# A Mamba layer with one-query attention on one core: filler products at the chunk borders, and jobs beside the scan moved by half states

## What is computed

```python
x = x + mamba(keep_largest_rows(x, sigmoid(cond @ score_w)))
x = x + ffn(attention(x, cond, mask))

# mamba, per sequence, 512 inner channels, 16 states
xi, z = split(rmsnorm(x) @ in_proj)
xi    = silu(causal_conv4(xi) + conv_b)
dt, Bm, Cm = split(xi @ x_proj)
delta = softplus(dt @ dt_w + dt_b)
h_s   = exp(delta * A_s) * h_s(before) + (delta * xi) * Bm_s     # 16 states s
y     = sum_s(h_s * Cm_s) + xi * D
out   = x + (y * silu(z)) @ out_proj

# attention: the same query for all rows of a sequence
qmod  = sum over rows of (tp . q) q ;  tp = cond @ Wt
o     = softmax(qmod . k) v @ Wo
```

## Time and profile before

| | |
|---|---|
| three runs | 529.36 us median (528.08 to 532.32) |
| the profiled execution, its own time | 528.79 us |
| its span, first to last instruction | 527.0 us |
| mean granted TensorE clock, as a share of full speed | 0.950 |
| before the loop's first scan | 42.88 us |
| chunks 0, 1, 2, 3 (first scan to first scan) | 113.10, 107.12, 103.77, 100.04 us |
| after the last scan | 60.09 us |

### The profile page before, as it was taken

One profiled execution on the slowest core, in us unless ns is written; L12 is line 12 of the kernel. 1 busy time (PEld: TensorE's weight loads), 2 busy tenths in 40 slices (PEclk: granted clock), 3 DMA queues, 4 the chain that ended last, 5 costly groups with the idle time before them and its releaser, 6 DMA issues.

```text
span 527.0 us, 8185 instructions
## 1 busy us (share of the span) xinstructions
PE 446.8 (85%) x2881; PEld 336.5 (64%) x2881; DVE 448.4 (85%) x527; ACT 380.3 (72%) x673; POOL 382.2 (73%) x235
## 2 busy tenths in 40 slices
PE   7967798887958999989789999896899778989991
PEld 6443665565648656766676667665888666878750
DVE  3779799989998899999998999999997998871153
ACT  4685688899966798898867988998676788741210
POOL 5139967986999579879996799799977999620001
PEclk9998899998997999999989999999997898899996
DMA  8531111111103111110110111101200295019205
GB/s 274 169 123 40 42 40 41 40 45 40 41 0 115 40 46 42 39 45 0 42 58 29 47 55 44 54 7 35 81 40 1 64 363 225 1 40 360 71 1 164
DMA packets 18422, 39.58 MB, mean 75 GB/s; under 512 B 1943, under 2 KB 10775, under 8 KB 18376
## 3 DMA queue, kind: packets, MB, share of 16 engines
q1 hardware_dynamic: 18376, 39.00, 21.3%
HBM read 36.76 MB, written 2.23 MB: 74 GB/s over the span
## 4 chain that ended last, share of the span: by engine, by line
PE 37%; DVE 34%; issue 16%; ACT 11%; POOL 1%; DVEq 0%; ACTq 0%; POOLq 0%
DVE scanmem L1951 22%; PE hT L974 7%; DVE yTd L1962 6%; PE pp L597 4%; PE pp L698 4%; PE yacc L668 4%; ACT dA L1442 3%; PE dA L936 2%; ACT hc L1452 2%; PE pp L766 2%; DVE yTd L1876 2%; PE pp L620 1%; PE pp L908 1%; PE pp L627 1%; DVE par L1742 1%
## 5 line engine op out<-in xcount | busy, mean ns | idle before, releaser
L1604 POOL TENSOR_TENSOR scanmem<-par,scanmem 128x1024 f32<-128x1024 f32 x128 | 300.1, 2365 | 57.6 <-PE hT L974 37.9
L974 PE MATMUL hT<-con,scanmem 128*128 128x128 f32 x1008 | 158.1, 287 | 49.3 <-DVE yTd L1962 35.5
L1442 ACT ACTIVATE dA<-par,Aneg 128x512 f32<-128x512 f32 x256 | 171.7, 690 | 36.0 <-DVE scanmem L1951 34.5
L974 PEld LDWEIGHTS hT<-con,scanmem 128*128 128x128 f32 x1008 | 118.1, 146 | 95.5 <-DVE yTd L1962 31.5
L1951 DVE TENSOR_TENSOR_SCAN scanmem<-dA,carry,scanmem 128x512 f32<-128x512 f32 x128 | 156.4, 1266 | 9.5 <-ACT dA L1442 8.1
L1951 DVE TENSOR_TENSOR_SCAN scanmem<-dA,scanmem 128x512 f32<-128x512 f32 x128 | 148.8, 1204 | 4.9 <-ACT dA L1442 3.2
L1452 ACT ACTIVATE hc<-hT,CTs 128x512 f32<-128x512 f32 x127 | 86.1, 678 | 25.4 <-PE hT L974 24.0
L668 PE MATMUL yacc<-con,hc 128*128 128x128 f32 x512 | 83.7, 290 | 0.0
L1962 DVE SCALAR_TENSOR_TENSOR yTd<-hT,CTs,yTd 128x512 f32<-128x512 f32 x90 | 65.4, 727 | 4.9 <-PE hT L974 2.5
L668 PEld LDWEIGHTS yacc<-con,hc 128*128 128x128 f32 x512 | 65.9, 151 | 0.2
L597 PE MATMUL pp<-xnT,wi 128*128 128x512 f32 x120 | 57.8, 609 | 4.1 <-DVE par L1742 2.4
(11 more groups left out here) (229 smaller groups left out, 527.9 us busy)
## 6 DMA issues: line engine op xcount, KB each, us to landing
scanmem<-brow SPq DMA_DIRECT2D x32, 512.0 KB, 3.6
par<-in SPq DMA_DIRECT2D x1, 4096.0 KB, 19.3
scanmem<-in SPq DMA_DIRECT2D x1, 4096.0 KB, 14.3
xt<-in SPq DMA_DIRECT2D x4, 512.0 KB, 6.9
wi<-in SPq DMA_DIRECT2D x2, 1024.0 KB, 7.9
out<-par SPq DMA_DIRECT2D x3, 512.0 KB, 3.9
aw<-in SPq DMA_DIRECT2D x5, 256.0 KB, 7.6
xr<-in SPq DMA_DIRECT2D x1, 1024.0 KB, 10.0
```

The costliest lines, as they stand in the source:

```text
L974: last = nc.tensor.transpose(hT[:, i % 2, m * P:(m + 1) * P], hb[:, n % RING, m, i * P:(i + 1) * P], ident)
L1442: A(dA[:, m % 2, :], delta(c)[:, m, :], ACT.Exp, scale=Aneg[:, m * NS + s:m * NS + s + 1]).then_inc(da_ready, 1)
L1604: nc.gpsimd.tensor_tensor(hb[:, n % RING, ms, :], dx(c)[:, ms, :], Bb[:, row:row + 1, :].to_broadcast([P, 2, T]), ALU.mult).then_inc(bx_re ...
```

## The change

The hand-written tables are changed; no product of the computation itself is added or left out.

1. In chunks 1 and 2 the next chunk's rows are turned at half 2 where it was half 3, and the first input product comes at half 3 where it was half 4 (`LATER_ROWS`).
2. A new job KW: six products of the identity with itself, 128x128, into the job's bank, read by nobody (the fifth frees the bank). It stands at halves 29, 31 and 32 of chunk 0 and at 31 and 32 of chunks 1 and 2 (half 32 is half 0 of the next chunk): seven jobs, 42 products.
3. U is moved from half 3 to half 30 of chunk 0.
4. `kept_rows` on POOL is moved from step 16 to step 18.
5. In chunk 3 the four O jobs stand one by one at halves 4, 5, 6 and 7 (it was two and two at 4 and 6), and A, G, A, G follow at 8, 9, 10, 11 (it was 7, 8, 8, 10).
6. SP waits for the last O in place of the second pair before it loads `H1` (its queue comes to that place after all of chunk 3's B rows).

```diff
+LATER_ROWS = {2: [("T", 0), ("T", 1)], 3: [("I", 0)], 4: [], 5: [("I", 1)]}
-LAST_EPILOGUE = {1: [("Y", 1)], 2: [("Y", 3)], 4: [("O", 0)], 6: [("O", 1)], 17: [("R", 0)], 19: [("R", 1)]}
-ATT = [7, 8, 8, 10, 12, ...
+LAST_EPILOGUE = {1: [("Y", 1)], 2: [("Y", 3)], 4: [("O", 0)], 5: [("O", 2)], 6: [("O", 1)], 7: [("O", 3)], 17: [("R", 0)], 19: [("R", 1)]}
+ATT = [8, 9, 10, 11, 12, ...
-KEPT_AT = NS
+KEPT_AT = NS + 2
+IDLE_AT = [(29, 31, 32), (31, 32)]
 def prologue_slots(n):
-    return slots(PROLOGUE if n > 1 else {**PROLOGUE, **FIRST_STEPS}, n)
+    return slots({**PROLOGUE, **(LATER_ROWS if n > 1 else FIRST_STEPS)}, n)
...
-            beside[3] += [("U", 0, 0)]
+            beside[30] += [("U", 0, 0)]
...
+            for k, h in enumerate(IDLE_AT[min(c, 1)]):
+                beside[at + h] += [("KW", c, k)]
...
+WARM_IDLE = 6
...
-            wait_full(sp, ("O", NCH - 2, 1))
+            wait_full(sp, ("O", NCH - 2, NT - 1))
...
+            def job_KW(job, o):
+
+                keep_warm(WARM_IDLE - 2, o[:, 0:P])
+                mm(o[:, 0:P], ident, ident, start=True, stop=True).then_inc(freed(job), 1)
+                return mm(o[:, P:2 * P], ident, ident, start=True, stop=True)
```

More of the change, by code:

```diff
@@ L58 @@
 FIRST_STEPS = {17: [("XT", 0)], 18: [("D", 0)], 19: [("D", 1)], 20: [], 21: [("D", 2)], 22: [("D", 3)]}
+LATER_ROWS = {2: [("T", 0), ("T", 1)], 3: [("I", 0)], 4: [], 5: [("I", 1)]}
 EPILOGUE = {1: [("Y", 1), ("Y", 3)], 15: [("O", 0)], 17: [("O", 2)], 18: [("O", 1)], 23: [("O", 3)], 28: [("R", 0)], 30: [("R", 1)]}
-LAST_EPILOGUE = {1: [("Y", 1)], 2: [("Y", 3)], 4: [("O", 0)], 6: [("O", 1)], 17: [("R", 0)], 19: [("R", 1)]}
-ATT = [7, 8, 8, 10, 12, 14, 15, 16, 18, 20, 22, 23, 25, 26, 28]
+LAST_EPILOGUE = {1: [("Y", 1)], 2: [("Y", 3)], 4: [("O", 0)], 5: [("O", 2)], 6: [("O", 1)], 7: [("O", 3)], 17: [("R", 0)], 19: [("R", 1)]}
+ATT = [8, 9, 10, 11, 12, 14, 15, 16, 18, 20, 22, 23, 25, 26, 28]
 ATT1 = [24, 27]
@@ L689, in job_O @@
                     pe.wait_ge(half_ready, 3)
[L690 to L698, removed]
+                t0 = j * P
+                if j % 2:
+                    wait_read(pe, ("Y", e, j))
+                else:
+                    pe.wait_ge(gated, 2 * e + j // 2 + 1)
+                for m in range(CT):
+                    last = mm(o[:, 0:DM], dx(e)[:, m, t0:t0 + P], wo[:, m, :], start=m == 0, stop=m == CT - 1)
                 return last
@@ L739, in job_R @@
                 wait_read(pe, ("O", e, j))
-                if e != NCH - 2:
-                    wait_read(pe, ("O", e, j + 2))
+                wait_read(pe, ("O", e, j + 2))
                 return turn_rows(o, e, j)
@@ L936, in keep_warm @@
                     mm(dst, ident, ident, start=True, stop=True)
+            def job_KW(job, o):
+                keep_warm(WARM_IDLE - 2, o[:, 0:P])
+                mm(o[:, 0:P], ident, ident, start=True, stop=True).then_inc(freed(job), 1)
+                return mm(o[:, P:2 * P], ident, ident, start=True, stop=True)
+            jobs["KW"] = job_KW
             def wait_free(job):
@@ L1762, in ev_O @@
                 _, e, j = job
[L1763 to L1766, removed]
+                g = e * NT + j
+                return V.scalar_tensor_tensor(xt[:, g, :], xt[:, g, :], keep1[:, g:g + 1], o[:, 0:DM], ALU.mult, ALU.add)
             def ev_AX(job, o):
```

## The result

| | before | after |
|---|---|---|
| median of 7 runs each | 530.05 us (526.81 to 532.32) | 524.65 us (522.73 to 525.63) |
| ratio | | 0.990, 95% interval 0.9868 to 0.9933 |
| profiled execution, span | 528.79, 527.0 us | 525.63, 523.8 us |
| mean granted clock | 0.950 | 0.954 |
| before the first scan | 42.88 us | 44.06 us |

The change makes the kernel 1.0% faster, 5.4 us between the medians; 523.9 had been forecast, a gain of 5.5 us on a median that was then 529.36. It loses 1.18 us ahead of the first scan and 1.30 us behind the last one (61.39 us, 60.09 before), where the change has touched nothing; the loop between them is 418.38 us, not 424.03, so 5.65 us shorter.

A forecast was written before the change was run, and what follows sets the result against it. No engine bounds it everywhere (VectorE and TensorE both 85% busy); VectorE's idle time inside the loop can be won. 0.9 + 1.17 + 0.9 + 0.5 + 2.4 - 0.4 = 5.5 us off 528.79, plus 0.57: 523.9 us, range 519.9 to 527.8.

The forecast's parts named there:

- U: Step 2: without U ahead of it T starts earlier and VectorE's wait for block 1 shrinks; 0.9 us, bounds 0.5 and 1.22.
- kept_rows: Step 15: with kept_rows behind POOL's sum, VectorE's whole wait for that sum goes; 1.17 us, bounds 0.6 and 1.17.
- The forecast's sentence on the clocks: Opening paragraph: granted clock 0.55 in step 16, 0.76 in step 32, 0.67 in step 52, 1.00 where nothing is said.
- Borders, T and I together: Chunk borders and following steps: 0.9 us gained at chunk 1's start, 0.5 at chunk 2's, less 0.4 for KW and U.
- The walk: Steps 32 to 35: T waits for VectorE to read Y; step 34 starts about 0.5 us later, step 35 at 284.0, not 284.24.
- the gate's waits: Steps 16 and 32: VectorE waits 0.76 and 0.73 us for the gate's sum; KW should hold the clock and remove both.
- Chunk 3: Step 52: spreading O, A and G wins 2.4 us of VectorE's 3.24 us wait; bounds 0.7 and 3.4.
- the rule: Step 52: transposes don't count for the clock as products do, so the low clock is sure and the term 1.6 us.
- All 3.24 us are won: Step 52 at the full clock: block 0 is there at 395.5 and VectorE's whole wait goes; 3.24 us.
- T is not held: Rival, steps 17, 18, 33, 34: Y's banks don't hold T, stalls go almost whole; 3 us more gain, 520.9 us, chance 0.17.
- The border products lie on the path: Rival, chunk borders: KW at low clock delays block 0, about 3 us per border; 536.8 or 530.0 us, chance 0.08.
- The spread doesn't lift step 52: Rival, steps 52 and 53: clock falls behind each A, only 0.7 us of chunk 3 won; 525.6 us, chance 0.25.

The follow-up runs named there:

- e5: The changed kernel with kept_rows back ahead of step 16 and U back at half 3; 525.66 us, ratio 0.9957 to the kernel before.
- e4: The changed kernel with chunk 3's O, A, G and SP's wait as in the kernel before; 525.18 us, ratio 0.9917 to the kernel before.
- e2: The changed kernel with T back at half 3 and the first input product at half 4; 524.59 us, ratio 0.9898 to the kernel before.
- e6: The changed kernel with GT, the turning of g, at half 13, not 12; 523.29 us, ratio 0.9908 to the kernel before.
- e3: The changed kernel without the seven KW jobs; 526.80 us, ratio 0.9944 to the kernel before.
- e11: The changed kernel with T and I back, GT at half 13 and chunks 1 and 2's convolution products a half or a state later; 525.27 us, ratio 0.9909.

## Why the prediction was right

The time was 0.8 us off and the gain 0.1, but as a sum whose terms erred in both directions: the borders were put too low and chunk 3 too high. The mechanisms of U, of `kept_rows` and of T held by Y were right; that the total fits so well is in part luck.

- **U, 0.9 us forecast:** 0.84 measured (e5 against e4). The forecast's sentence on the clocks leaves step 2 at 1.00; its row has 0.89, and the term itself reckoned with that. In the profile of after it is covered by 5.0 us of low clock in step 1, which is 9.55 us long (8.55 before). Both e4 and e5 have 2.0 us of low clock in step 2; what U costs at the full clock was not measured.
- **kept_rows, 1.17 forecast:** 1.27 measured, nothing given back.
- **Borders, T and I together, 0.9 + 0.5 - 0.4 = 1.0 forecast:** 1.33 in chunk 1 and 1.14 in chunk 2, less 0 to 0.5 at the border of chunks 2 and 3, so about 2.2. The step that failed is the split: "Chunk 2's start gains 0.2 + 0.3 = 0.5 us. By the same walk chunk 1's start gains 0.9". The walk itself was right in kind: T is held by Y for 1.25 us, the first scan of step 34 waits 1.39, the stall behind I is smaller. It was too dark in size: from the start of step 32, step 34 starts 0.27 us later than before (forecast 0.5) and step 35 0.59 earlier (forecast 0.24), and step 35 itself is 0.55 shorter (forecast 0.3). And I set the gate's waits of 0.76 and 0.73 us against the late start and took the rest as T's gain. With T left late (e2) the gain is larger, 1.56 and 1.25, so it is KW's, up to the 0.3 of chunk 1 named above: besides the gate's wait the idle time behind it goes too, and step 17 is 6.49 us in e2 and was 7.17. Beside KW, T and I early cost 0.33. I also charged 0.2 for the two KW in steps 14 and 15; those stages are 5.73 and 5.76 us, as short as VectorE's work.
- **Chunk 3, 2.4 forecast:** 0.4 to 1.7 measured. For step 52 the number was right: 9.03 to 6.33, 2.7 us, with the clock at 1.00 around A, and step 50 gave 0.39 more that no term had. By the rule in the Trainium skill, page "TensorE: Matmul & The Clock Gate", section "Part 4: PE-mode transpose", the clock should have been low there; step 52 is at 1.00 in all eleven profiles with the spread. In the kernel before, PE did nothing but transposes from 356.16 to 371.82 us, at 1.00 throughout. So here the measurement decides against the rule. What failed is "All 3.24 us are won" as an end: I followed A and stopped at step 53, while the same table moved the second G next to GT. That costs 0.86 us with the clock at 1.00 and 2.00 with it at 0.66, and e6 takes it away.

The rivals: *T is not held* is refuted by the 1.25 us that PE waits for VectorE. *The border products lie on the path* is refuted by e3, which is slower without them. *The spread doesn't lift step 52* is wrong on step 52, yet its price, 1.7 us less, was nearly right in three of the six profiles with this table, for another reason.

By the terms, 0.84 + 1.27 + 2.2 + 0.4 to 1.7 is 4.7 to 6.0 us; the medians say 5.4.

The two profiles themselves bear the sum out less well than the medians. Of the 5.65 us by which the loop is shorter, the stages that the forecast names (1, 2, 15, 16 to 19, 32 to 35, 47, 50 to 54) give 3.75. The other 1.9 lie in steps 28, 44 and 56 to 63, whose work the change leaves alone: step 28 is 6.35 us, 7.12 before, and steps 56 to 63 are 47.47, 48.84 before. They follow the clock: step 28 is 7.12 or 7.13 us in the four profiles with a clock of 0.91 to 0.93 in it, and 6.34 to 6.62 in the ten at 1.00.

## What to carry to other kernels

When a hand-written order is changed, walk on to the next job that needs the result of the one moved: two dependent jobs in neighbouring slots are a wait, however short they are, if a third engine reads the first in between. When two edits aim at the same stretch, measure the four combinations; the edit that named this change gained nothing once the other was in. And where VectorE's idle time keeps its sum under the orders tried, as in steps 33 to 35 under three (a fourth, e11, made it worse), look elsewhere first.

## What was not expected of the hardware

Where the granted clock falls can cost more than most of these edits gain. The same head gave steps 1 and 2 together 15.77 us (e2, clock 1.00 in them) and 18.58 (after, 6.8 us of low clock). Of twelve profiles that issue the same work in chunk 0's steps 10 and 11, five had the low clock in both, 13.65 us of it, and lost 3.1 us or a little more over steps 11, 12 and 15; in the others only step 10 had it and nothing was lost. In those steps PE waits 1.43 and 1.61 us close together. Six products put into the first wait left 0.81 and 0.85 us of waiting, and the clock stayed at 1.00 in both profiles that had them, where each of the twelve had some low clock in step 10. How often it is low in runs that were not profiled was not measured.
